# A graph network kernel on one core: x in three requests, the first chunk begun behind the first gather, the second chunk begun in half columns

## The reference

```
x: (1250, 512);  src, dst: 21250 edges, sorted by dst (20000 random ones and one loop per node)
eps, W1 (512, 1024), W2 (1024, 512), b, g, be: layer 0;  lw1 (512, 256), lb1, lw2 (256, 512), lb2: layer 1

layer 0:  agg = segment_sum(x[src], dst)
          h = (1 + eps) * x + agg
          h = relu(batch_norm(h @ W1 + b1, g1, be1))
          h = relu(batch_norm(h @ W2 + b2, g2, be2))
          x1 = layernorm(x + x + h)
layer 1:  h = relu(x1 @ lw1 + lb1) @ lw2 + lb2
          out = layernorm(x1 + h + segment_sum(h[dst], src))
```

## Time and profile before

| | |
|---|---|
| median of the runs | 249.6 us |
| the profiled execution | 249.95 us, its span 248.1 us |
| busy in the span | PE 231.0 us (93%), DVE 156.2 (63%), ACT 134.2 (54%), POOL 88.0 (35%) |
| granted TensorE clock, mean | 0.995 |
| chain that ended last | PE 70%, DVE 12%, DMA 7%, ACT 6% |

### The profile page before, as it was taken

The page is one execution under the profiler, slowest core; times in us unless marked ns, Lnnn a source line. Parts: engine busy times, 40 slices in busy tenths (PEclk is TensorE's granted clock), DMA queues, the critical chain, the costliest instruction groups (busy, mean ns, idle before and its releaser), DMA issues.

```text
span 248.1 us, 3897 instructions
## 1 busy us (share of the span) xinstructions
PE 231.0 (93%) x1454; PEld 197.3 (80%) x1454; DVE 156.2 (63%) x362; ACT 134.2 (54%) x233; POOL 88.0 (35%) x83
## 2 busy tenths in 40 slices
PE   0858999999999999999999999999999999999990
PEld 0845997777888888888888888888889997888970
DVE  1669899873966344555544316264876899796374
ACT  0656774763868067444455504457471639936373
POOL 5420000004920006565554500423456459701251
PEclk9999999999999999999999999999999999999998
DMA  3467800000066501111000087503209920000334
GB/s 100 156 214 214 202 0 3 1 3 3 3 261 239 198 1 45 42 42 45 0 0 0 4 206 142 106 3 60 45 4 170 202 85 3 0 0 0 131 127 160
DMA packets 32323, 19.96 MB, mean 80 GB/s; under 512 B 21927, under 2 KB 27084, under 8 KB 32302
## 3 DMA queue, kind: packets, MB, share of 16 engines
q1 hardware_dynamic: 31796, 19.45, 28.6%
q0 software_dynamic: 160, 0.13, 0.2%
q10 hardware_dynamic: 346, 0.10, 0.2%
HBM read 8.51 MB, written 5.92 MB: 58 GB/s over the span
## 4 chain that ended last, share of the span: by engine, by line
PE 70%; DVE 12%; DMA 7%; ACT 6%; issue 2%; POOL 1%; SPq 1%; DVEq 0%
PE ps L1281 22%; PE ps L1220 17%; PE ps L1298 11%; PE ps L1344 9%; PE ps L1362 6%; PE ps L1311 3%; DVE hot_s L849 3%; DMA plane_T<-planes 2%; PE ps L1200 2%; DMA src_i<-in_src 2%; DVE xT L984 2%; DMA pairs<-pair 2%; ACT planes L715 1%; DVE small_t L942 1%; DMA run<-pairs,start_i 1%
## 5 line engine op out<-in xcount | busy, mean ns | idle before, releaser
L942 DVE BATCH_NORM_STATS2 small_t<-ps 128x6 f32<-128x500 f32 (+1 forms) x36 | 21.6, 599 | 38.7 <-PE ps L1281 25.2
L1220 PE MATMUL ps<-AT,xh 128*128 128x500 f32 (+2 forms) x120 | 42.6, 366 | 0.4 <-ACT AT L569 0.4
L1220 PE MATMUL ps<-AT,xl 128*128 128x500 f32 (+2 forms) x120 | 40.9, 352 | 0.0
L1281 PE MATMUL ps<-h0h,wh 128*128 128x500 f32 (+1 forms) x96 | 33.9, 353 | 0.0
L1281 PE MATMUL ps<-h0h,wl 128*128 128x500 f32 (+1 forms) x96 | 33.9, 353 | 0.0
L1281 PE MATMUL ps<-h0l,wh 128*128 128x500 f32 (+1 forms) x96 | 33.8, 352 | 0.0
L485 POOL TENSOR_TENSOR wl<-w2s,wh 128x512 fp32r<-128x512 f32 x8 | 11.1, 1384 | 43.9 <-ACT wh L689 43.9
L480 POOL TENSOR_TENSOR wl<-w1s,wh 128x512 fp32r<-128x512 f32 x8 | 10.1, 1301 | 45.7 <-ACT AT L569 45.7
L1220 PEld LDWEIGHTS ps<-AT,xh 128*128 128x128 f32 (+1 forms) x120 | 22.6, 188 | 3.3 <-ACT AT L569 0.6
L1220 PEld LDWEIGHTS ps<-AT,xl 128*128 128x128 f32 (+1 forms) x120 | 22.7, 189 | 2.7
L1298 PE MATMUL ps<-a1h,wh 128*128 128x500 f32 (+1 forms) x96 | 23.7, 355 | 0.0
(11 more groups left out here) (148 smaller groups left out, 508.2 us busy)
## 6 DMA issues: line engine op xcount, KB each, us to landing
turns<-half_out SPq DMA_DIRECT2D x10, 320.0 KB, 2.2
out<-x SPq DMA_DIRECT2D x9, 256.0 KB
w1s<-in_L_gnn_W SPq DMA_DIRECT2D x4, 512.0 KB, 7.1
w2s<-in_L_gnn_W SPq DMA_DIRECT2D x8, 256.0 KB, 2.7
xs<-in_x SPq DMA_DIRECT2D x1, 1280.0 KB, 7.9
xs<-in_x SPq DMA_DIRECT2D x1, 1024.0 KB
lws<-in_L_gnn_W SPq DMA_DIRECT2D x1, 512.0 KB, 4.0
lw2s<-in_L_gnn_W SPq DMA_DIRECT2D x1, 512.0 KB, 4.2
```

What stands on the lines that cost most here:

```text
L942: link(nc.vector.bn_stats(stats[:, 6 * c:6 * c + 6], ps[:, zbank(t, c), 0:c1 - c0]))
L1220: last = mm(o, part[0:r, k, d * P:d * P + P], AT[0:r, k, c0:c1], start=(k == 0 and j == 0), stop=(k == NT - 1 and j == 1))
L1281: last = mm(ps[:, zbank(t, c), 0:c1 - c0], w[:, t, d * P:d * P + P], h[c][:, d, :], start=(d == 0 and j == 0), stop=(d == DT - 1 and j == 2))
```

## The change

- SP: x is loaded in three steps: tiles 0 and 1 at the start, 2 to 4 when the packing is done (`pair_set`), 5 to 9 as before behind the gathers' requests.
- VectorE: `below` and `edge_row` stand ahead of `pair`; the copy of `par` waits for `pair_out`; xl of tiles 0 and 1 only stands ahead of the gathers, that of tile 2 in the keys, those of 3 to 9 in slots 5 to 11.
- The first five groups take the windows in another order: first the 25 windows c = 0, then the 25 windows c = 1 of the first 250 destinations. So groups 0 and 1 need the first gather alone, group 2 both. Keys are made for these 25 columns first (`early_keys`), for the other 100 behind the five groups (`late_keys`). ScalarE's copy writes pieces of 5 columns, in two instructions for group 2.
- ScalarE: a copy of one column at the start, which brings the table load with it.
- Tile 6 is transposed in slot 5, so tiles 6 to 9 are in slots 5 to 8.
- The first chunk's 40 units now stand in slots 5 to 14 as 5, 5, 5, 5, 5, 5, 3, 3, 2, 2. Slots 11 to 14 also have 5 units each of results 4 and 5 for their first 250 columns alone; the other 250 columns, and results 6 and 7 whole, are in slots 15 to 24, four units a slot.

The diff, cut:

```diff
@@ tables
+        HALF_COLS = CH[0][1]
+        HALF_READY = (CH[1][0] + HALF_COLS) // (WG * WIN)
+        SPLIT = RING - DT
+        first = [(d, k, None) for k in range(NT) for d in range(DT)]
+        left = [(DT + d, k, 0) for k in range(NT) for d in range(SPLIT)]
+        second_units = [(DT + d, k, 1) for d in range(SPLIT) for k in range(NT)]
+        second_units += [(DT + d, k, None) for d in range(SPLIT, DT) for k in range(NT)]
+        first_per, left_per = [5] * 6 + [3, 3, 2, 2], [0] * 6 + [5] * 4
...
-        cols_at = {6: half + 2, 7: half + 3, 11: half + 4}
+        cols_at = {5: half + 1, 6: half + 2, 7: half + 3, 8: half + 4}
...
-        low_at = {7: half, 10: half + 1, 11: half + 2, 12: half + 3, 13: half + 4}
-        early_cols = {EARLY - 3: half, EARLY - 1: half + 1}
+        low_at = {5 + j: XA + 1 + j for j in range(NT - XA - 1)}
+        early_cols = {EARLY - 2: half}
@@ SP
-            sp.dma_start(xs[:, 0:half, :], x[0:half * P, :].rearrange("(t p) d -> p t d", p=P)).then_inc(x_in, 16)
+            sp.dma_start(xs[:, 0:XA, :], x[0:XA * P, :].rearrange("(t p) d -> p t d", p=P)).then_inc(x_in, 16)
+            sp.wait_ge(pair_set, 1)
+            sp.dma_start(xs[:, XA:half, :], x[XA * P:half * P, :].rearrange("(t p) d -> p t d", p=P)).then_inc(x_mid, 16)
             sp.wait_ge(runs_asked, 1)
@@ ScalarE
+            act.wait_ge(const, 5)
+            nc.scalar.activation(asked[:, :], ones[:, :], ACT.Copy).then_inc(table_set, 1)
             act.wait_ge(pair_set, 1)
             act.dma_start(pairs.rearrange("(p f) -> p f", p=ER), pair[0:ER, :]).then_inc(pair_out, 16)
...
             for g in range(EARLY):
-                group_out(g)
-                if g in early_cols:
-                    x_turn(early_cols[g])
+                early_out(g)
+            for k in early_cols.values():
+                x_turn(k)
@@ VectorE
             v.wait_ge(par_T, 1)
+            v.wait_ge(pair_out, 16)
             nc.vector.tensor_copy(par[:, :], ps[:, 2, 0:3 * BT]).then_inc(par_set, 1)
...
+            shifted(0)
+            x_low(XA)
+            early_keys(0)
+            early_hots(0)
+            shifted(1)
+            early_hots(1)
+            early_keys(1)
+            early_hots(2)
+            early_hots(3)
...
+            early_hots(4)
+            late_keys(0)
+            late_keys(1)
@@ TensorE, aggregate
+                p0 = HALF_COLS if h == 1 else 0
+                p1 = HALF_COLS if h == 0 else c1 - c0
+                o = ps[:, 2 + i % RING, p0:p1]
...
+                    pe.wait_ge(AT_set, HALF_READY if h == 0 else CHG[c])
...
+                    if k == 0:
+                        pe.wait_ge(keys_read, 1)
```

More of the change, by code:

```diff
@@ new lines, in gnn_kernel @@
+        slot_units = [[] for _ in range(NG)]
+        for j in range(CHG[1] - CHG[0]):
+            a, b = sum(first_per[:j]), sum(left_per[:j])
+            slot_units[CHG[0] + j] = first[a:a + first_per[j]] + left[b:b + left_per[j]]
+        for j, u in enumerate(second_units):
+            slot_units[CHG[1] + j * (CHG[2] - CHG[1]) // len(second_units)].append(u)
+        assert sum(first_per) == len(first) and sum(left_per) == len(left) and len(CH) == 3
+        assert all(CHG[0] + j > HALF_READY for j, n in enumerate(left_per) if n)
@@ L1168, in _ @@
             nc.tensor.transpose(ps[:, 2, 0:3 * BT], par_r[0:3 * BT, :], ident[0:3 * BT, 0:3 * BT]).then_inc(par_T, 1)
-            for k in range(half):
+            for k in range(XA + 1):
                 x_cols(k)
@@ L1175, in between, with keys @@
                 for _ in range(n):
-                    mm(ps[:, x_bank(0), 0:2 * P], flat[:, 0:P], flat, start=True, stop=True)
-            pe.wait_ge(const, 6)
-            pe.wait_ge(xT_set, 1)
-            for c in range(2):
-                pe.wait_ge(rel_set, c + 1)
-                nc.tensor.transpose(ps[:, c, 0:NW], rel[0:NW, c * RUN:(c + 1) * RUN], ident[0:NW, 0:NW]).then_inc(rel_T, 1)
-                between((4, 7)[c])
+                    mm(ps[:, fill_bank, 0:2 * P], flat[:, 0:P], flat, start=True, stop=True)
+            def keys(c):
+                pe.wait_ge(*((par_set, 1) if c == 0 else (xT_set, half)))
+                pe.wait_ge(rel_set, c + 1)
+                nc.tensor.transpose(keys_at(c, 0, NW), rel[0:NW, c * RUN:(c + 1) * RUN],
+                                    ident[0:NW, 0:NW]).then_inc(rel_T, 1)
+            pe.wait_ge(const, 6)
             def count():
@@ L1214, in aggregate @@
                     else:
-                        pe.wait_ge(xT_set, half)
+                        pe.wait_ge(xT_set, half + 1 if 2 + i == x_bank(half) else half)
                 if i == 0:
                     pe.wait_ge(xl_set, k + 1)
+                    if k == 0:
+                        pe.wait_ge(keys_read, 1)
                 r = rows[k]
                 for j, part in enumerate((xh, xl)):
-                    last = mm(o, part[0:r, k, d * P:d * P + P], AT[0:r, k, c0:c1], start=(k == 0 and j == 0),
-                              stop=(k == NT - 1 and j == 1))
-                if k == NT - 1:
+                    last = mm(o, part[0:r, k, d * P:d * P + P], AT[0:r, k, c0 + p0:c0 + p1],
+                              start=(k == 0 and j == 0 and h != 1), stop=(k == NT - 1 and j == 1),
+                              skip_group_check=(h is not None))
+                if k == NT - 1 and h != 0:
                     last.then_inc(h0_sum, 1)
-            for g in range(EARLY):
-                build(g)
-                if g == 0:
-                    count()
-                if g in early_cols:
-                    x_cols(early_cols[g])
-                elif g < EARLY - 1:
-                    between((2, 4, 4, 4)[g])
+            keys(0)
+            for k in range(XA + 1, half):
+                x_cols(k)
+            pe.wait_ge(xT_set, fill_bank - 2)
+            between(2)
+            build(0)
+            keys(1)
+            between(3)
+            build(1)
+            count()
+            between(4)
+            build(2)
+            between(4)
+            build(3)
+            x_cols(early_cols[3])
+            build(4)
             pe.wait_ge(flag_set, 1)
@@ L1266, in _ @@
                 pe.wait_ge(AT_set, NG)
-                for u in units[0:(len(CH) - 1) * per]:
+                for u in first + left + second_units:
                     aggregate(*u)
```

109 lines of the change are left out of this document (73 added, 36 removed).

## The result

The changed kernel takes 252.87 us (252.5 to 253.16, 6 runs), the kernel before 250.02 (249.52 to 250.54, 6 runs) beside it: ratio 1.0113 [1.0096, 1.0131]. It is 2.85 us slower, where I had forecast 1.4 us faster. The profiled spans are 251.1 and 248.1 us, the granted clocks 0.999 and 0.995.

The account below looks back on a forecast made before the run. DMA latency, GpSimd's requests and VectorE fill the first 24 us; behind them TensorE bounds. -2.2 to the first aggregation, +0.25 in the first chunk, +0.55 in slots 15 to 19: -1.4 from 249.6, 248.2 us; 8-in-10 range 246.9 to 250.0.

Parts of the forecast that it names:

- Part 1: Start to the gathers: pair write takes 2.5 us and lands at 8.6; first gather lands at 12.9 against 14.16.
- the first rival: Pair write shares its engines packet for packet with x tiles 2 to 4, landing at 11.3; 250.9 us, chance 0.13.
- Part 2: First gather to first aggregation: first one-hots at 14.4 against 17.29, first aggregation at 21.9, -2.2 us.
- T0: Start of the first aggregation on TensorE, 24.10 us in the kernel before; forecast at 21.9.
- Part 3: First chunk's slots: half columns fill waits, a 0.9 us wait for one-hots 6 and tile 6 put them back; +0.25 us.
- Part 4: Slots 15 to 19: VectorE needs 9.0 us against TensorE's 6.1, one-hots 20 come after build 20 could start; +0.55 us.
- From slot 20 on both programs issue the same instructions with the same slack: From the build of slot 20 (49.81 us before) to the end, the rest moves rigidly, with no further change.
- 2 (ScalarE in slots 5 to 9): ScalarE's xh slips 0.3 us in four slots, xl waits, VectorE and TensorE lose 1.2 us; 249.4 us, chance 0.17.
- 3: More gain: first gather request 1.30 us, pair write 2.2, VectorE keeps up in slots 15 to 19; 247.0 us, chance 0.15.
- 4 (the clock): TensorE's clock falls to 1.2 GHz before the first aggregation, costing 1.9 us; 250.1 us, chance 0.05.

Follow-up runs that it names:

- e7: Changed kernel with x tiles 2 to 4 requested only when the pair write has landed; 252.35 us, ratio 1.0092.
- e4: Changed kernel with x tiles 2 to 4 requested right behind tiles 0 and 1, not behind the packing; 252.90 us, ratio 1.0113.
- e6: Changed kernel with 48 never-executed matmuls added to the branch that is not taken; 252.51 us, ratio 1.01.
- e8: Changed kernel with VectorE's load of the flag ahead of the late keys instead of behind them; 251.73 us, ratio 1.0066.
- e3: Changed kernel without half columns, four whole units in each of slots 5 to 24; 251.63 us, ratio 1.0078.
- e9: Changed kernel with xl of x tiles 3 and 4 moved into VectorE's idle stretch before the first gather lands; 251.77 us, ratio 1.0069.
- e2: Kernel before the change with 40 never-executed matmuls added to the branch that is not taken; 251.75 us, ratio 1.0065.
- e10: Changed kernel with TensorE's aggregation units taken out of the branch that is not taken; 250.93 us, ratio 1.0037.
- e1: Changed kernel with 20 whole units in place of 40 half-column ones in the branch not taken; 252.65 us, ratio 1.0104.
- e11: Changed kernel with the edits of e3, e8 and e9 together; 250.01 us, ratio 0.9997 to the kernel before.
- e12: e11 with tile 6 transposed before the first aggregation and xl of tiles 6 to 9 at slots 9, 10, 12, 13; 248.98 us, ratio 0.9956.

## Why the prediction was wrong

**Part 1, the pair write: this step failed.** I took 2.5 us of write and a landing at 8.6; it took 3.48 and landed at 10.05. The mechanism was the first rival's: the write shares with tiles 2 to 4, and e7 shows it by taking the sharing away (2.21 us). The rival's price was wrong too: I had let the pairs wait for all 24 packets of x on their engines, giving 11.3. My argument against it was that the later x request of the kernel before had needed 2 us to reach its full rate. But its packets do not wait for that. Issued at 13.81, the first run at 14.90 us; the view from 14.5 to 15.0 has six:

```profile
q1 hardware_dynamic: 6, 0.01, 16.6%
```

In the changed kernel both requests are issued at 6.57; the pair's packets start at 7.35 and those of x at 7.63. From 7.35 to 9.65 us it has:

```profile
q1 hardware_dynamic: 215, 0.44, 61.7%
q10 hardware_dynamic: 129, 0.09, 15.6%
```

So full rate was the wrong sign to read; the first packet was the right one. The pair's packets are done at 9.63, where alone (e7) they take from 7.20 to 8.22. The start of the write was 0.45 us late as well, which I don't explain: src takes 5.02 us to land (the chain's DMA src_i), 4.65 to 5.04 in the nine other kernels of this front where the chain names it, and 4.36 to 4.46 in the three profiles with the old front, though it is the same request in the same place. But wherever x is under way beside or ahead of the write, it lands at 9.8 to 10.2, whether it is issued at 6.20 (e4, 3.96 us) or at 6.59 (e6, 3.41 us). It looks as if x sets the landing more than the start does; no run moves the start alone.

**Part 2, from the landing to T0: right.** I had 13.3 us from the landing of the pairs to T0; it took 13.30. GpSimd's 1.88, the gather, the keys and the late keys within the last 1.33 us all came as worked out. The whole miss of 1.45 us at T0 is the landing's.

**Part 3, T0 to build 15: right in kind, 0.95 us too low.** I took 19.75, it took 20.70. The wait for one-hots 6 is there (0.76 for my 0.9), but build 5 waits too, 0.24, and both builds come 0.5 us later than I put them: I had left out the load of the flag, which the late keys now lay bare for 0.8 us (e8 gives it back). The other 0.4 is, as far as the rows show, the price of a matmul: the chain has 1.25 us for ten of 250 columns, where I had taken 0.118 us for each. That I called this "+0.25" hid the larger fact: the half columns fill waits that the change itself makes. VectorE got two more xl and the keys behind T0 and lost its lead (e3, e9).

**Part 4, slots 15 to 19: right**, +0.7 for +0.55, with the wait at build 20 of 0.41.

**"From slot 20 on both programs issue the same instructions with the same slack": wrong**, and as costly as the landing. The instructions are the same, but they stand elsewhere. I had put nothing at all for the jump. It takes 0.42 us before and 3.70 us changed, because with the longer program it has to wait for a fetch: 1.55 us of idle TensorE, 1.70 by starts, and 1.6 to 1.7 in the time (e2, e10). The trace of the kernel before has the jump only as 0.42 us of the sequencer, which is hidden; the sign was in the diff, which puts 20 units (40 matmuls with their weight loads) more in each branch.

**The rivals.** 1 was right in mechanism and half right in price. 2 (ScalarE in slots 5 to 9) fell: one wait of VectorE for xh, 0.17 us. 3 fell with the landing. 4 (the clock) fell: these stretches of the changed kernel, to set beside the earlier trace rows, have a granted clock of 1.00, the higher level of 2.4 GHz:

```profile
0.00:10.00 10.00, 3.81 (x16) 3.69 (x17) 2.72 (x11) 2.95 (x5) 4.87 (x21) 1.00 0.49 136
13.85:18.50 4.65, 3.61 (x26) 3.29 (x27) 3.90 (x11) 2.02 (x6) 0.01 (x1) 1.00 0.74 249
```

So three things make the 4.4 us between the forecast (-1.4) and the profiled spans (+3.0): the landing (1.45), the jump (1.7), the flag and the matmuls' price behind T0 (0.95); the slots behind 15 add 0.3.

**What stays open.** When the jump's target is already fetched: e1, whose untaken branch is as long as in the kernel before but stands some 80 instructions later, has the stop, and e3, e11 and e12, with a branch of that length too, have jumps of 1.40, 0.42 and 1.73 us. Neither length nor place alone decides, and no run separates the rest. Nor is it known why the same packet of 16 KB takes 0.96 us in one kernel and 1.36 in another.

## What to carry to other kernels

Look for an engine that is idle early and the bound later (here VectorE: 2.9 us idle before the gather, the pace of TensorE after it). Moving work into its idle stretch and off its busy one brought 0.75 us at build 15 in e9, and a cheaper place for the flag's load 0.84 in e8. Together with leaving out the half columns, which removed the stop, and the two moves of e12, this turned a change that lost 2.85 us into one that gains 1.1 to 1.3. When work is split to fill waits, ask first who makes the waits. And when a program gets longer around a branch, count the jump as a possible stop of over 1 us, even if nothing that runs near it has changed; the duration of the branch instruction shows it where the named releaser doesn't.

## What was not expected of the hardware

- The same taken jump on TensorE takes 0.2 to 3.7 us of its sequencer, by whether it waits for a 16 KB packet of instructions. About 2 us of that are hidden here; the rest, 1.2 to 1.55 us of idle engine, the profile puts down to a semaphore (h0l) or to "issue".
- A flag's load into VectorE's queue costs next to nothing behind a 0.8 us operation (e8) and 0.8 us behind short ones that wait for each other (the changed kernel).
- A write of 83 KB from 125 partitions takes 2.21 us alone (e7) and 3.4 to 4.0 beside or behind a stream of x.
